# Where the tokens of a block are transposed, and a block more between a block and its experts, in the third layer of a graph network

## The chip, the cores and the metric

The program runs on one core of one Trainium2 chip. The metric is the device time of one execution in microseconds (us), the median over several. The core has five engines with queues of their own: TensorE (PE in the profile; PEld are its weight loads), VectorE (DVE), ScalarE (ACT), GpSimd (POOL) and SyncE (SP). They wait for one another by semaphores.

## The reference

6250 nodes with 256 features, 206250 edges sorted by target, 8 edge types. All is in fp32. The kernel computes

```
xn = layernorm(x)
h = xn
for l in 0, 1, 2:                      # graph network
    agg[r, n] = sum of h[src] over the edges of type r to node n
    h = einsum('rnd,rde->ne', agg, W[l]) + h @ root[l] + bias[l]
    h = relu(h) if l < 2 else sigmoid(h)
x = x + h + mixer(xn)                  # mixer: linear attention and an MLP
t = layernorm(x)
probs = softmax(t @ router.T); the two largest, scaled to sum 1, are combine
y = t + sum over 8 experts e of combine[e] * (gelu(t @ w1[e] + b1[e]) @ w2[e] + b2[e])
out = x + y
```

## The kernel before

**Tiles and stages.** The nodes are cut into 50 blocks (`window`) of 125. Before each layer a table of the nodes' features, already multiplied by the eight matrices of the edge types, lies in HBM; a layer is then a gather of rows and a sum by target. The first stage (phase 0) makes the table for layer 0; layers 0 and 1 make the next one, block by block. Layer 0 also does the mixer's projections, layer 1 its MLP, and layer 2, the third, the router and the experts.

**The gathers.** GpSimd issues one indirect DMA for each 128 edges (`nc.gpsimd.indirect_dma_start`, L517), 1612 a layer. Four of them are a chunk. Chunks go round in a ring of 8 slots in SBUF; before each chunk GpSimd waits on `slots_free`. SyncE turns landed halves of chunks into counts of `halves_ready`.

**A block's sum.** VectorE compares the edges' targets with the block's 125 nodes (`onehot`, L1022), and TensorE multiplies that with the gathered rows, four matrix products a chunk (`unit`, `add_tile` L1434). A block has seven units of fixed place, 0 to 6, and in a loop before the last one as many more as its edges need (`more_units`); the chunk of a block's last unit is also the first one of the next block. The first product of a unit frees the slot of the unit before it. When unit 6 is done VectorE adds what was computed beside it (`summing`, L1070).

**The third layer.** For the sum of block w: ScalarE takes the sigmoid as a tanh (`squash`, L795). VectorE adds the rest of the node, does the layer norm by Newton steps and gives the tokens `xhat` (`layer_out`, L1238 to L1251, semaphore `t_ready`). TensorE transposes them into `ps_tr` (`tokens_transposed`, which calls `transform`, L1377), ScalarE copies that to `hT` (L580). Then come the experts in six parts on TensorE (`experts(win, part)`): part 0 is the router's logits (L1689) and the up projections of experts 0 and 1 (L1699), parts 1 to 5 the other ups and the down projections (L1710), with the transposed combine weights (L1717) and the bias (L1722) among them. ScalarE does the router's exponential (L799), a Gelu for each half of an up projection (L810) and a table load at each change between Exp and Gelu; `warm` (L574) brings the Exp table early. VectorE finds the router's two largest (`largest_logit`, `router`, L1256 to L1279) and adds the experts into the block's output (`take`, L1289). ScalarE issues the store (L820).

**Order.** No scheduler is at work. Each engine runs its own queue in the order in which the code is written, so what stands behind a wait waits too. In block w of the third layer TensorE has unit 0, 1, 2, the transposes of block w-1, unit 3, part 0 of w-1, unit 4, parts 1 and 2, unit 5, parts 3 and 4, the extra units, unit 6, part 5. When the last block's units are done, `phase3_tail` does the last block's transposes and its six parts. ScalarE and VectorE have bodies of their own (`phase3`, `phase3_tail`), in which the work of block w-1 stands in the matching order.

Of the kernel before, what the change touches and what calls it, by code (L numbers as in the profile page):

```python
# [22 lines left out]
ACT = mybir.ActivationFunctionType  # L23
# [14 lines left out]
def gps_program(nc, t):  # L38
# [35 lines left out]
    with ExitStack() as ctx:  # L74
# [449 lines left out]
        def _(act):  # L524
# [252 lines left out]
            def phase3(cur, prev):  # L777
                w, parity, turn = cur
                load_base(2, w, parity)

                act.dma_start(xn_in[parity][:, :], rows(res_dram, w)).then_inc(xn_loaded[parity], 16)
                if w == 0 or w >= 2:
                    warm(ACT.Exp)
                if prev:
                    squash(prev)
                    copy_hT(3, prev)
                    logits_exp(prev)
                    gelus3(prev, range(E))
                    if w < NW - 1:
                        store_out(prev)  # L790

            def squash(win):

                act.wait_ge(summed, 2 * NW + win[0] + 1)
                nc.scalar.activation(h_sum[:, :], h_sum[:, :], ACT.Tanh, scale=0.5).then_inc(tanh_ready, 1)  # L795
# [25 lines left out]

            def experts(win):
                logits_exp(win)
                gelus3(win, range(E))
                store_out(win)

            def phase3_tail(win):
                warm(ACT.Exp)
                squash(win)
                copy_hT(3, win)  # L830
                logits_exp(win)
                store_out(window(win[0] - 1))
                gelus3(win, range(E))
                store_out(win)
# [6 lines left out]
        def _(dve):  # L841
# [388 lines left out]
            def layer_out(cur):  # L1230
# [4 lines left out]
                dve.wait_ge(tanh_ready, w + 1)  # L1235
                dve.wait_ge(xn_loaded[parity], turn * 16 + (16 + 2 * 16 * (NW // 2)))

                chain(nc.vector.scalar_tensor_tensor(out=fx[:, :], in0=h_sum[:, :], scalar=0.5,  # L1238
# [64 lines left out]
            def phase3(cur, prev, step):  # L1303
                step(3)
                if prev:
                    assert layer_out(prev) == P3_CHAIN
                step(4, 5)
                if prev:
                    largest_logit(prev)
                    router(prev)  # L1310
                    take(prev, range(0, 4))
                    take_b2(prev)
                step(6)
                if prev and cur[0] < NW - 1:
                    take(prev, range(4, E))

# [10 lines left out]
            def phase3_tail(win):  # L1327
                assert layer_out(win) == P3_CHAIN
                take(window(win[0] - 1), range(4, E))
                whole_block(win)  # L1330
# [4 lines left out]
        def _(pe):  # L1335
# [347 lines left out]
            def experts(win, part):  # L1683
# [9 lines left out]
                def up(e):  # L1693

                    if e >= 2:
                        pe.wait_ge(act_done, w * E + (e - 1))
# [55 lines left out]

            PARTS_BEHIND = {3: (0,), 4: (1, 2), 5: (3, 4), 6: (5,)}

            def phase3(cur, prev, unit):
                w = cur[0]
                for i in range(STATIC):
                    if i == STATIC - 1:
                        more_units(2, w)
                    unit(i)  # L1760
                    if prev and i == 2:
                        tokens_transposed(prev)
                    if prev:
                        for part in PARTS_BEHIND.get(i, ()):
                            experts(prev, part)

            def phase3_tail(win):
                tokens_transposed(win)
                for part in range(6):
                    experts(win, part)  # L1770
# [21 lines left out]
```

## Time and profile before

| | |
|---|---|
| three timed runs | 6509.38, 6512.33, 6513.76 us; median 6512.33 |
| profiled execution, first to last instruction | 8038.5 us |
| TensorE, products | 5658.1 us, 70% |
| GpSimd | 4625.1 us, 58% |
| VectorE | 2215.5 us, 28% |
| ScalarE | 1034.0 us, 13% |
| layer starts (first gather) | 386.8, 2853.1 and 5358.6 us |

The profiled execution has no other time than its span. It is 1526 us longer than the median, so it isn't a picture of the timed runs in every wait. Starts of TensorE's instructions are recorded, their ends are modelled. GpSimd's rows are the issues of gathers, not the transfers. A releaser called "remote" is one that the profile can't name, and "issue" is time in which it sees no wait at all.

### The profile page before, as it was taken

To read this page: it belongs to the slowest core of one execution; us is meant where nothing else is said; L and a number is where in the kernel's file an instruction comes from. 1 tells how busy PE (TensorE), PEld (TensorE's weight loads), DVE (VectorE), ACT (ScalarE), POOL (GpSimd) and SP (SyncE) were. 2 spreads that over 40 slices of the span, in tenths; PEclk is the share of its full clock that TensorE was granted. 3 is DMA by queue.
4 is the path that set the end of the run, shared out by engine and by line. 5 is a ranking of instruction groups with operands and counts; after the bars stand their busy time and mean duration, and the time that the engine had idled before them with its cause. 6 is when DMAs were issued, how large, how long until landed. Compare 5 with 4: busy or idle time off the path is not lost.

```text
span 8038.5 us, 86017 instructions
## 1 busy us (share of the span) xinstructions
PE 5658.1 (70%) x22890; PEld 4136.2 (51%) x22890; DVE 2215.5 (28%) x6194; ACT 1034.0 (13%) x2706; POOL 4625.1 (58%) x4920
## 2 busy tenths in 40 slices
PE   8946666666656677777777777766676666766667
PEld 3434444444444445555555555545565555555556
DVE  8711111111111122222222222213333333333333
ACT  2200000000001011111111111111111111111112
POOL 1166666666666656666666666655555555555554
PEclk9977887788778888888888888888888888888888
DMA  6633333333333344344444444443233333323332
GB/s 189 189 102 110 113 112 110 115 115 114 114 114 112 115 127 117 116 121 120 120 119 117 119 120 119 124 128 88 86 87 89 89 89 88 89 87 89 91 88 67
DMA packets 354391, 888.01 MB, mean 110 GB/s; under 512 B 86234, under 2 KB 179294, under 8 KB 335623
## 3 DMA queue, kind: packets, MB, share of 16 engines
q0 software_dynamic: 232080, 633.91, 26.9%
q10 hardware_dynamic: 114178, 243.16, 10.4%
q1 hardware_dynamic: 7740, 5.99, 0.2%
q8 instruction: 212, 3.47, 0.2%
q14 instruction: 181, 1.48, 0.1%
HBM read 697.11 MB, written 185.60 MB: 110 GB/s over the span
## 4 chain that ended last, share of the span: by engine, by line
PE 39%; another core or an unknown queue 32%; issue 15%; DVE 6%; ACT 4%; ACTq 2%; DVEq 1%; DMA 1%; POOL 0%; POOLq 0%; SPq 0%
PE ps_out L1434 16%; PE ps_y L1405 7%; PE ps_y L1699 4%; PE ps_b L1710 3%; PE ps_c L1710 2%; PE ps_tr L1614 2%; DVE r L1289 1%; DVE onehot L1022 1%; PE ps_b L1405 1%; PE ps_c L1405 1%; PE ps_c L1602 1%; ACT L810 1%; ACT L574 1%; PE ps_b L1602 1%
## 5 line engine op out<-in xcount | busy, mean ns | idle before, releaser
L517 POOL DMA_INDIRECT ring<-table,gather_idx x4836 | 4576.4, 946 | 3030.0 <-issue 1391.3
L1434 PE MATMUL ps_out<-ring,onehot 128*125 x8400 | 2148.6, 403 | 261.6 <-issue 221.5
L1434 PEld LDWEIGHTS ps_out<-ring,onehot 128*125 128x125 f32 x8400 | 1625.0, 200 | 653.8 <-issue 415.8
L1434 PE MATMUL ps_out<-ring,onehot_more 128*125 x2448 | 783.2, 476 | 832.0 <-DVE onehot_more L1022 596.0
L1405 PE MATMUL ps_y<-W,hT 128*125 128x512 f32 (+1 forms) x2400 | 1138.8, 615 | 170.9 <-issue 69.7
L1434 PEld LDWEIGHTS ps_out<-ring,onehot_more 128*125 128x125 f32 x2448 | 550.1, 236 | 1036.1 <-issue 937.8
L1405 PEld LDWEIGHTS ps_y<-W,hT 128*125 128x125 f32 x2400 | 496.2, 210 | 677.8 <-issue 552.1
L849 DVE COPY y_stage<-ps_y 125x512 f32<-125x512 f32 x150 | 103.6, 690 | 2174.5 <-remote 1231.6
L1022 DVE TENSOR_TENSOR onehot<-targets,ps_out 128x500 f32<-128x500 f32 x1050 | 647.2, 671 | 180.8 <-issue 138.8
L1022 DVE TENSOR_TENSOR onehot_more<-targets,ps_out 128x250 f32<-128x250 f32 x612 | 239.8, 414 | 1016.2 <-remote 416.7
L533 ACT COPY y_stage<-ps_y 125x512 f32<-125x512 f32 x350 | 201.1, 587 | 2455.3 <-PE ps_y L1405 1165.7
L1699 PE MATMUL ps_y<-hT,big 128*128 128x125 f32 x3200 | 472.3, 302 | 42.4 <-ACT gT L810 26.8
L1699 PEld LDWEIGHTS ps_y<-hT,big 128*128 128x128 f32 x3200 | 457.3, 217 | 76.9 <-issue 33.2
L1377 PE MATMUL ps_tr<-ident,xhat 125*128 125x125 f32 x100 | 32.7, 428 | 530.8 <-issue 436.9
L1710 PE MATMUL ps_b<-big,gT 128*125 128x256 f32 x800 | 243.2, 432 | 133.7 <-ACT gT L810 132.5
L810 ACT ACTIVATE gT<-ps_y,vectors 128x125 f32<-128x125 f32 x800 | 242.6, 363 | 600.3 <-PE ps_y L1699 401.5
L1377 PEld LDWEIGHTS ps_tr<-ident,xhat 125*128 125x128 f32 x100 | 14.1, 198 | 554.1 <-issue 453.9
L1289 DVE SCALAR_TENSOR_TENSOR r<-ps_c,combine,r 125x256 f32<-125x256 f32 x200 | 96.8, 484 | 564.7 <-remote 318.4
L1710 PEld LDWEIGHTS ps_b<-big,gT 128*125 128x125 f32 x800 | 157.7, 214 | 169.7 <-issue 142.4
L1289 DVE SCALAR_TENSOR_TENSOR r<-ps_b,combine,r 125x256 f32<-125x256 f32 x200 | 96.8, 484 | 536.3 <-PE ps_b L1710 149.7
L490 POOL TENSOR_TENSOR rstd<-mv,neg_half 125x1 f32<-125x1 f32 x50 | 33.4, 667 | 313.6 <-DVE mv L969 313.6
L1614 PE MATMUL ps_tr<-big,gT 128*125 128x256 f32 x800 | 187.4, 388 | 27.3 <-issue 27.1
(193 smaller groups left out, 3643.0 us busy)
## 6 DMA issues: line engine op xcount, KB each, us to landing
table<-y_stage ACTq DMA_DIRECT2D x147, 896.0 KB
ring<-table,gather_idx POOLq DMA_INDIRECT x4836
table<-y_stage ACTq DMA_DIRECT2D x147, 104.0 KB
xn_in<-xn_scratch ACTq DMA_DIRECT2D x100, 125.0 KB
base<-y_stage ACTq DMA_DIRECT2D x100, 125.0 KB
base_in<-base ACTq DMA_DIRECT2D x100, 125.0 KB
x_in<-in_x_dram ACTq DMA_DIRECT2D x75, 125.0 KB
xn_scratch<-xn_in ACTq DMA_DIRECT2D x50, 125.0 KB
```

What stands on the lines that cost most here:

```text
L517: nc.gpsimd.indirect_dma_start(ring[0:n, c * D:(c + 1) * D], None, table[l], bass.IndirectOffsetOnAxis(ap=gather_idx[0:n, tile:tile + 1].b ...
L533: nc.scalar.copy(y_stage[parity][:, b * 2 * D:(b + 1) * 2 * D], BANK[phase][b][0:WIN, 0:2 * D]).then_inc(y_evac_act, 1)
L810: last = nc.scalar.activation(gT[:, (e % GB) * K + f, :], ps_y[e % 2][:, f * WIN:(f + 1) * WIN], ACT.Gelu, bias=b1e[:, e, f:f + 1])
L849: nc.vector.tensor_copy(y_stage[parity][:, 2 * D:4 * D], BANK[phase][1][0:WIN, 0:2 * D]).then_inc(y_evac_dve, 1)
L1022: return nc.vector.tensor_tensor(out, targets[:, bass.ds(col, count)].unsqueeze(2).broadcast_to([128, count, n]), nodes.unsqueeze(1).broad ...
L1289: nc.vector.scalar_tensor_tensor(out=acc[parity][:, :], in0=(ps_b, ps_c)[e // 2 % 2][0:WIN, e % 2 * D:(e % 2 + 1) * D], scalar=combine[:, ...
L1405: last = nc.tensor.matmul(BANK[phase][b][0:WIN, 0:n], hT[parity][:, k, :], W[:, k, b * 2 * D:b * 2 * D + n], start=(k == 0), stop=(k == K ...
L1434: return nc.tensor.matmul(ps_out[w % 2][0:WIN, 0:D], lhsT, ring[:, bass.ds(slot + j * D, D)], start=first, stop=last)
L1602: last = nc.tensor.matmul(bank[:, (j % 4) * WIN:(j % 4 + 1) * WIN], W1[:, k, j * 128:(j + 1) * 128], xhatT[:, k, :], start=(k == 0), stop= ...
L1614: last = nc.tensor.matmul(ps_tr[0:WIN, D:2 * D], gT[:, j, :], W2[:, j, :], start=(j == 0), stop=(j == FJ - 1))
L1699: last = nc.tensor.matmul(ps_y[e % 2][:, f * WIN:(f + 1) * WIN], w1e[:, e, k, f * 128:(f + 1) * 128], hT[parity][:, k, :], start=(k == 0), ...
L1710: last = nc.tensor.matmul((ps_b, ps_c)[e // 2 % 2][0:WIN, e % 2 * D:(e % 2 + 1) * D], gT[:, (e % GB) * K + f, :], w2e[:, e, f, :], start=( ...
```

## The change

In the third layer a block now has two blocks in work beside its own sums: `win`, the block before, up to its transposed tokens, and `old`, the one before that, for its experts. On TensorE block w now has unit 0, part 0 of w-2, unit 1, part 1, unit 2, part 2, unit 3, part 3, the transposes of block w-1, unit 4, part 4, unit 5, part 5, the extra units, unit 6. On ScalarE `both_blocks` does the exponential and two experts' Gelus of the older block, the tanh of the newer, five experts, the copy of the transposed tokens, the last expert and the store. On VectorE it does the router of the older block, the layer norm of the newer, the takes. The layer norm waits for the transposes of the block before it, since `xhat` is one buffer. In the tail of each engine stand first both blocks, 48 and 49, and then the experts of block 49.

```
@@ scalar, phase3
-                if w == 0 or w >= 2:
+                old = window(w - 2) if w >= 2 else None
+                if w == 0:
                     warm(ACT.Exp)
                 if prev:
-                    squash(prev)
-                    copy_hT(3, prev)
-                    logits_exp(prev)
-                    gelus3(prev, range(E))
-                    if w < NW - 1:
-                        store_out(prev)
+                    both_blocks(old, prev)
+
+            def both_blocks(old, win):
+
+                if old:
+                    warm(ACT.Exp)
+                    logits_exp(old)
+                    gelus3(old, range(0, 2))
+                squash(win)
+                if old:
+                    gelus3(old, range(2, E - 1))
+                copy_hT(3, win)
+                if old:
+                    gelus3(old, range(E - 1, E))
+                    store_out(old)
...
             def phase3_tail(win):
-                warm(ACT.Exp)
-                squash(win)
-                copy_hT(3, win)
+                both_blocks(window(win[0] - 1), win)
                 logits_exp(win)
-                store_out(window(win[0] - 1))
                 gelus3(win, range(E))
                 store_out(win)
@@ vector, layer_out
                 dve.wait_ge(xn_loaded[parity], turn * 16 + (16 + 2 * 16 * (NW // 2)))
+                dve.wait_ge(tr_done, 2 * NW + w)
@@ vector, phase3
-                step(3)
-                if prev:
-                    assert layer_out(prev) == P3_CHAIN
-                step(4, 5)
-                if prev:
-                    largest_logit(prev)
-                    router(prev)
-                    take(prev, range(0, 4))
-                    take_b2(prev)
+                old = window(cur[0] - 2) if cur[0] >= 2 else None
+                step(3, 4, 5)
+                if prev:
+                    both_blocks(old, prev)
                 step(6)
-                if prev and cur[0] < NW - 1:
-                    take(prev, range(4, E))
+                if old:
+                    take(old, range(4, E))
+
+            def both_blocks(old, win):
+
+                if old:
+                    largest_logit(old)
+                    router(old)
+                assert layer_out(win) == P3_CHAIN
+                if old:
+                    take(old, range(0, 4))
+                    take_b2(old)
...
             def phase3_tail(win):
-                assert layer_out(win) == P3_CHAIN
-                take(window(win[0] - 1), range(4, E))
+                old = window(win[0] - 1)
+                both_blocks(old, win)
+                take(old, range(4, E))
                 whole_block(win)
@@ tensor, experts: up(e)
-                    if e >= 2:
+                    if w * E + e >= 2:
                         pe.wait_ge(act_done, w * E + (e - 1))
@@ tensor, phase3
-            PARTS_BEHIND = {3: (0,), 4: (1, 2), 5: (3, 4), 6: (5,)}
-
...
                     unit(i)
-                    if prev and i == 2:
-                        tokens_transposed(prev)
-                    if prev:
-                        for part in PARTS_BEHIND.get(i, ()):
-                            experts(prev, part)
+                    both_blocks(old, prev, i)
+
+            def both_blocks(old, win, i):
+
+                if old and i < 6:
+                    experts(old, i)
+                if win and i == 3:
+                    tokens_transposed(win)

             def phase3_tail(win):
-                tokens_transposed(win)
+                for i in range(6):
+                    both_blocks(window(win[0] - 1), win, i)
                 for part in range(6):
                     experts(win, part)
```

The first place is in the middle of the third layer on TensorE, around the transposes (`ps_tr`). Before, between two units (`ps_out`):

```order
L1434 MATMUL ps_out<-ring,onehot 125x256
L1377 MATMUL ps_tr<-ident,xhat 128x125 x2
L1451 ISA
L1434 ISA
L1434 MATMUL ps_out<-ring,onehot 125x256
```

Now, behind part 3 of the older block (ups `ps_y`, a down `ps_c`, the bias `ps_a`):

```order
L1708 MATMUL ps_y<-hT,big 128x125 x4
L1719 MATMUL ps_c<-big,gT 125x256 x2
L1731 MATMUL ps_a<-b2e,combT 125x256
L1708 MATMUL ps_y<-hT,big 128x125 x4
L1386 MATMUL ps_tr<-ident,xhat 128x125 x2
L1460 ISA
```

The transposes have moved from behind the third unit to behind the fourth and the older block's part 3.

The second place is the end of the program on TensorE, from the last unit's last product. Before:

```order
L1434 MATMUL ps_out<-ring,onehot 125x256
L1710 MATMUL ps_b<-big,gT 125x256 x2
L1710 MATMUL ps_c<-big,gT 125x256 x4
L1377 MATMUL ps_tr<-ident,xhat 128x125 x2
L1689 MATMUL ps_a<-vectors,hT 125x8 x2
L1699 MATMUL ps_y<-hT,big 128x125 x8
```

Now, from the same product; what is left out are parts 1 to 3 of block 48:

```order
L1443 MATMUL ps_out<-ring,onehot 125x256
L1698 MATMUL ps_a<-vectors,hT 125x8 x2
L1708 MATMUL ps_y<-hT,big 128x125 x8
L1719 MATMUL ps_b<-big,gT 125x256 x2
...
L1386 MATMUL ps_tr<-ident,xhat 128x125 x2
L1719 MATMUL ps_b<-big,gT 125x256 x2
L1708 MATMUL ps_y<-hT,big 128x125 x4
L1719 MATMUL ps_b<-big,gT 125x256 x2
L1719 MATMUL ps_c<-big,gT 125x256 x4
L1698 MATMUL ps_a<-vectors,hT 125x8 x2
L1708 MATMUL ps_y<-hT,big 128x125 x8
```

One block of experts stood behind the last unit but for three downs; now two whole ones stand there.

The third place is the end of the program on ScalarE. Before (`probs` is the router's exponential, `out_dram` the store):

```order
L574 ACT_TABLE_LOAD
L574 ACTIVATE act_warm<-zero_col 128x1
L795 ACTIVATE h_sum<-h_sum 125x256
L580 ACTIVATE hT<-ps_tr 128x2x125
L799 ACTIVATE probs,small<-ps_a,small 125x8
L820 DMA out_dram<-r_0 125x256
L810 ACT_TABLE_LOAD
```

Now, from block 48's first two experts on:

```order
L820 ACTIVATE gT<-ps_y,vectors 128x125 x4
L805 ACTIVATE h_sum<-h_sum 125x256
L820 ACTIVATE gT<-ps_y,vectors 128x125 x6
L825 COPY combT<-ps_a 8x125
L820 ACTIVATE gT<-ps_y,vectors 128x125 x4
L580 ACTIVATE hT<-ps_tr 128x2x125
L820 ACTIVATE gT<-ps_y,vectors 128x125 x2
L830 DMA out_dram<-r_0 125x256
L809 ACT_TABLE_LOAD
L809 ACTIVATE probs,small<-ps_a,small 125x8
L820 ACT_TABLE_LOAD
```

The tanh (`h_sum`) stands between Gelus and has no table load of its own; block 49's exponential has one, behind the store.

## Rows read from the trace of the kernel before

**Rows 1.** The page's section 1: busy time of each engine, share of the span, instructions
```profile
PE 5658.1 (70%) x22890; PEld 4136.2 (51%) x22890; DVE 2215.5 (28%) x6194; ACT 1034.0 (13%) x2706; POOL 4625.1 (58%) x4920
```

**Rows 2.** The page's section 5, GpSimd's gathers: count | busy, mean ns | idle before, releasers
```profile
L517 POOL DMA_INDIRECT ring<-table,gather_idx x4836 | 4576.4, 946 | 3030.0 <-issue 1391.3
```

**Rows 3.** Timeline, GpSimd, end of the third layer: start, length, what [idle before <-releaser]
```profile
7972.99 0.95 POOL L517 DMA_INDIRECT ring<-table,gather_idx  x1 [0.30 <-issue]
7977.26 0.94 POOL L517 DMA_INDIRECT ring<-table,gather_idx  x1 [3.32 <-remote]
```

**Rows 4.** Timeline, GpSimd, the first gather of each layer
```profile
386.76 1.22 POOL L517 DMA_INDIRECT ring<-table,gather_idx  x1 [11.29 <-issue]
...
2853.07 0.98 POOL L517 DMA_INDIRECT ring<-table,gather_idx  x1 [28.99 <-issue]
...
5358.59 0.97 POOL L517 DMA_INDIRECT ring<-table,gather_idx  x1 [30.83 <-issue]
```

**Rows 5.** Groups of instructions, GpSimd, 5358 to 7982, the third layer
```profile
L517 POOL DMA_INDIRECT ring<-table,gather_idx x1612 | 1525.2, 946 | 1128.9 <-issue 449.6 <-PE ps_out L1434 367.5 <-remote 311.8
```

**Rows 6.** Timeline, TensorE and VectorE, around one block's transposes
```profile
6602.84 1.89 PE L1710 MATMUL ps_c<-big,gT 128*125 128x256 f32 x8
...
6604.56 5.34 PE L1434 MATMUL ps_out<-ring,onehot 128*125 x24
...
6614.27 1.00 DVE L1289 SCALAR_TENSOR_TENSOR r<-ps_c,combine,r 125x256 f32<-125x256 f32 x2 [8.31 <-remote]
...
6622.03 0.68 PE L1377 MATMUL ps_tr<-ident,xhat 125*128 125x125 f32 x2 [12.12 <-issue]
```

**Rows 7.** Timeline, TensorE, one block at full clock
```profile
6684.65 2.04 PE L1710 MATMUL ps_b<-big,gT 128*125 128x256 f32 x4 [3.47 <-ACT gT L810]
...
6691.49 1.89 PE L1434 MATMUL ps_out<-ring,onehot 128*125 x8
...
6707.53 5.34 PE L1434 MATMUL ps_out<-ring,onehot 128*125 x24
```

**Rows 8.** Waits, 5800 to 7900: who <- for what: us in total, times, longest
```profile
PE ps_tr L1377 <- issue: 378.9, 32, 12.4
```

**Rows 9.** Timeline, all engines, the end of the program
```profile
8009.01 1.99 PE L1434 MATMUL ps_out<-ring,onehot 128*125 x8 [0.34 <-issue]
...
8015.71 0.44 PE L1377 MATMUL ps_tr<-ident,xhat 125*128 125x125 f32 x2 [2.12 <-DVE xhat L1245]
...
8016.71 0.57 PE L1689 MATMUL ps_a<-vectors,hT 128*125 128x8 f32 x4 [0.56 <-ACT hT L580]
...
8017.14 2.03 PE L1699 MATMUL ps_y<-hT,big 128*128 128x125 f32 x16
...
8018.23 0.17 DVE L1256 TENSOR_REDUCE small<-ps_a 125x1 f32<-125x8 f32 x1
8018.43 0.27 ACT L799 ACTIVATE probs<-ps_a,small 125x8 f32<-125x8 f32 x1 [1.86 <-DVE small L1256]
...
8018.80 1.28 ACT L810 ACT_TABLE_LOAD   x1
...
8020.10 1.13 ACT L810 ACTIVATE gT<-ps_y,vectors 128x125 f32<-128x125 f32 x4
...
8020.86 1.10 PE L1710 MATMUL ps_b<-big,gT 128*125 128x256 f32 x4 [1.70 <-ACT gT L810]
...
8032.40 1.89 PE L1710 MATMUL ps_c<-big,gT 128*125 128x256 f32 x8
...
8035.43 0.27 ACTq L820 DMA_DIRECT2D out_dram<-r  x1
```

**Rows 10.** Stretches: start:end, length, busy us (x) of PE, PEld, DVE, ACT, POOL, PEclk, DMA, GB/s
```profile
6614.00:6626.00 12.00, 3.97 (x11) 3.13 (x12) 7.33 (x22) 2.17 (x4) 8.47 (x9) 0.50 0.40 117
...
8011.00:8038.50 27.50, 18.91 (x117) 15.89 (x116) 12.58 (x42) 7.54 (x22) 0.00 (x0) 1.00 0.03 10
5700.00:7900.00 2200.00, 1533.89 (x7418) 1271.55 (x7417) 719.25 (x2101) 372.63 (x1002) 1279.05 (x1353) 0.83 0.31 89
```

More of the change, by code:

```diff
@@ L820, in store_out, with phase3_tail @@
                 act.dma_start(rows(t["out"], w), acc[parity][:, :]).then_inc(out_stored[parity], 16)
-            def experts(win):
+            def phase3_tail(win):
+                both_blocks(window(win[0] - 1), win)
                 logits_exp(win)
-                gelus3(win, range(E))
-                store_out(win)
-            def phase3_tail(win):
-                warm(ACT.Exp)
-                squash(win)
-                copy_hT(3, win)
-                logits_exp(win)
-                store_out(window(win[0] - 1))
                 gelus3(win, range(E))
@@ L1751, in experts @@
                         down(e)
-            PARTS_BEHIND = {3: (0,), 4: (1, 2), 5: (3, 4), 6: (5,)}
             def phase3(cur, prev, unit):
                 w = cur[0]
+                old = window(w - 2) if w >= 2 else None
                 for i in range(STATIC):
```

## The prediction

> **What bounds the kernel now.** I read the page first: TensorE is busy 5658.1 us of 8038.5, GpSimd 4625.1 [rows 1]. By that alone TensorE bounds the kernel. But the profiled span is 1526 us longer than the median of 6512.3 us, and no other time of that execution is given. So I first ask what in the trace is not in the timed runs.
>
> GpSimd issues all 4836 gathers, four to a chunk, and stands idle 3030.0 us between them [rows 2]. Its own timeline shows two kinds of gap: 0.30 us behind nearly every gather, so that one takes 0.95 + 0.30 = 1.25 us, and some longer ones, 3.32 us before the gather at 7977.26 [rows 3]. The long ones are waits for a free slot of the ring, which TensorE frees. The regular gaps are 4836 x 0.30 = 1451 us; the starts of the three layers are 11.3 + 29.0 + 30.8 = 71 us [rows 4]. What is left, 3030.0 - 1451 - 71 = 1508 us, are waits on TensorE. Take them out of the span: 8038.5 - 1508 = 6530 us, against 6512.3 measured. The timed runs are as long as the trace without a single one of these waits. From this I conclude that unprofiled the gathers' pace of 1.25 us bounds all three layers, and that TensorE's lateness belongs mostly to the profiled execution.
>
> The trace supports that where the wait of the third layer stands. TensorE's records end the last three experts' down projections at 6602.84 + 1.89 = 6604.7, and three units at 6604.56 + 5.34 = 6609.9; yet VectorE gets the last experts' result only at 6614.27, after 8.31 us of waiting for something unnamed, and the transposes begin at 6622.03, 12.1 us behind the units [rows 6]. Multiplications that the records price at 1.89 us have become about 9.5 us late. On its chain from there, VectorE and ScalarE need 6622.03 - 6614.27 = 7.8 us to make the tokens.
>
> The Trainium skill, "NOTIFIC — the notification-queue block", section 7.1, says that the block through which profiling records leave has a mode that stalls the engine producing them, "Stall the producer until software drains the ring", and that its inner pipeline always holds back rather than lose one. That would explain the lateness; by that rule it goes away unprofiled. No run here shows the mechanism.
>
> **TensorE against the gathers, third layer.** At full clock, from the first down projection of a block (6684.65) to the next block's first three units (6707.53) are 22.9 us, two extra units in it; those three units take 5.3 us [rows 7]. Transposes 0.44, the fourth unit 1.89, logits 0.57, two up projections 2.03 and the fifth unit 1.89 make 6.8 us [rows 7, 9]. Together 35.0 us. The chain of 7.8 us has 5.3 us of units beside it, so 2.4 us of real wait: 37.4 us a block. The gathers of a block take 1612 / 50 x 1.25 = 40.3 us. TensorE has 2.9 us a block to spare before the change, and eight chunks, 40 us of gathers, to even out its bursts.
>
> **The change part by part.**
> In blocks 2 to 49 of the third layer the transposes move from behind the third unit to behind the fourth and three quarters of the older block's experts. What waited 12 us there in the trace (378.9 us over the 32 waits of one kind that a stretch of 2200 us shows [rows 8]) now has about 15 us of other work in front. In the trace this is a large gain: the third layer's waits for slots are 1128.9 - 1612 x 0.30 - 30.8 = 614 us [rows 4, 5]. Unprofiled the 2.4 us a block go away behind a pace of 40.3 us that is not TensorE's: value 0. If the cover were gone (TensorE the bound), it would be worth 48 x 2.4 = 115 us; the bound from the other side is 0.
>
> VectorE builds two onehots before the router and no longer behind the tokens, and waits in addition for the previous transposes. Behind that new wait are the layer norm, the takes and the sixth onehot; the transposes that it waits for ended a whole block earlier: 0. ScalarE does two Gelu experts before the tanh; its table loads stay two a block, since the tanh stands behind Gelu without a load of its own: 0 in the loop. The bare move of the DMA store of an output block by one block is hidden by the alternating buffers: 0. GpSimd's and SyncE's queues have the same instructions in the same order.
>
> The end of the program has no gathers left to hide anything. Call U the end of the last unit, 8009.01 + 1.99 = 8011.0 in the trace; the span ends 27.5 us later, at 8038.5 [rows 9]. Before, three down projections stood there beside the last block's tanh and layer norm, and then one block of experts. Now TensorE has to do all of block 48's experts and then all of block 49's, and ScalarE and VectorE have both too:
> - U to block 48's first down projection. Logits 0.57 and two ups 2.03 are 2.6. The other way round, logits 0.57 and 0.3 to VectorE, then 8018.23 to 8020.86 (maximum, exponential, table load 1.28, Gelu) are 2.63 [rows 9]: 3.5 us. Block 49's layer norm runs under it.
> - From there to the last down projection's end, 8034.29 - 8020.86 = 13.4, and the transposes 0.44: 13.9 us.
> - Block 49's first down projection can't follow at once. ScalarE's queue has block 48's store in front of the exponential, and that waits for VectorE's last two takes: 8034.29 to 8035.70 are 1.4 us. A load of the Exp table follows, 1.28 us, which before was done early under TensorE's work. Then 8018.43 to 8020.86, 2.4 us. With the hand-over 5.2 us, under which TensorE's logits and first ups hide.
> - From there to the end of the span: 8038.5 - 8020.86 = 17.6 us.
> The sum is 3.5 + 13.9 + 5.2 + 17.6 = 40.2 us behind U, 27.5 before: +12.7 us.
>
> On that table load the Trainium skill, "ScalarE: Activation LUTs", section "What ACT_TABLE_LOAD costs", gives 1283 ns and a drain of about 1380 ns more for each switch. The trace has the 1.28 but lets the Gelu begin at 20.10, straight behind 18.80 + 1.28; the row decides. By the page the end would be an estimated 1.4 us longer.
>
> U itself. After the change TensorE has caught up before the last block ends: two extra units and the last one each wait for chunks 5 us apart and need 2.0. Where it waited long, the granted clock was 0.50 (1.2 GHz) between 6614 and 6626; over the last 27.5 us, with waits of about 2 us, it was 1.00 [rows 10]. At half clock the second half of the last unit and the first 2.6 us of experts would cost up to 3.5 us more; at full clock 0. Most of the last stretch is nearer to the second row; I take 1. Before the change TensorE is later in the last block by up to 2 us (five parts behind two units), so U may come that much earlier now: I take 0, keep -2. In all +13.7 us, between +10.7 and +16.2. On the profiled span alone the end would be 8052, but there the steady part falls; on the median it is 6512.3 + 13.7 = 6526.
>
> **Rivals.**
> A. The end is paid, but U comes 2 us earlier and the clock holds: +10.7 us, 6523, within 0.2%. For it: full clock through the end of the trace. Against it: TensorE's short work between chunks.
> B. Not slower: TensorE does bound part of the third layer. If a gather took 1.22 us unprofiled and not 1.25, the timed runs would hold 145 us of waits; by the trace's share of the third layer (614 of 1508) 59 us would lie there, and taking 2.4 us of each block's wait out of the way would return 60% of them, -35 + 13 = -22: 6490. It decides from TensorE's 37.4 us a block being above the gathers' time, which asks for a pace under 1.16, or for half clock in a fifth of the block. For it: the clock was 0.83 in the layer in the trace [rows 10]. Against it: the gaps of 0.30 never shrink, and the sum above closes within 18 us without any wait.
> C. The trace taken at its word, 379 us less for the third layer's wait: 6512 - 379 + 13 = 6146. Against it: 4836 x 1.25 = 6045 us of gathers, and 387 us before the first one [rows 4], are 6432 already. Impossible if the pace holds.
> D. The two blocks' experts at the end run at half clock throughout, or the moved order makes GpSimd wait: +13 for the order and +7 for a quarter of the engine's 27 us at half clock: 6532.
>
> **How the numbers follow.** Forecast 0.49, A 0.31, B 0.10, C 0.01, D 0.09. About 0.2%, 13 us, is what a measurement of this kernel can tell from no change. Slower by over 13.0 us (above 6525.4): most of the forecast's spread and D, less what of the forecast falls below, 0.52. Within: A and the rest, 0.38. Faster: B and C, 0.10. The range 6505 to 6537 takes in the bounds of the end and the weaker half of B; for the forecast alone it is 6522 to 6530.
>
> **What would show it.** In the profile of the changed kernel: the gathers' regular pace still 1.25; the wait before the transposes gone or under 2 us; the third layer's waits of GpSimd clearly under 614 us, and the profiled span so perhaps shorter by 100 us or more, while the median is longer; two runs of experts behind the last unit, 40 to 43 us from its end to the end of the span, an Exp load behind the store in ScalarE's queue between them. I am wrong if the median falls under 6500, since then TensorE was the bound unprofiled, or if the end is long and the median unchanged, since then there was a gain in the loop that I don't see.

## The result, and the profile after

| | us, median | lowest to highest | runs |
|---|---|---|---|
| before | 6512.25 | 6509.38 to 6515.15 | 12 |
| after | 6526.93 | 6523.42 to 6529.55 | 12 |

The ratio is 1.0023, with a 95% interval from 1.0015 to 1.0030: 14.7 us slower, where 6526 and +13.7 us were forecast. The profiled execution of after has a span of 6523.7 us, 3 us under its median, so here the profile is a picture of the timed runs. That of before was not, at 8038.5. Two groups of the page of after answer to [rows 1] and [rows 2]; the columns are the same.

```profile
PE 5464.6 (84%) x22890; PEld 3995.9 (61%) x22890; DVE 2201.3 (34%) x6194; ACT 1041.3 (16%) x2706; POOL 4631.4 (71%) x4920
```
```profile
L517 POOL DMA_INDIRECT ring<-table,gather_idx x4836 | 4582.9, 948 | 1520.8 <-issue 1466.0
```

A gather takes the same 0.95 us, but the idle time between gathers is 1520.8 us and not 3030.0. The difference is 1509 us; the prediction had counted 1508 us of waits for TensorE and taken them out of the sum. The page's chain of waits, which for before named TensorE with 39% of the span, now names the gathers (the row's end is left out):

```profile
POOL ring L517 54%; DMA ring<-table,gather_idx 9%; PE ps_out L1443 7%; PE ps_y L1414 3%; PE ps_y L1708 2%; DVE hT L980 1%; PE ps_b L1414 1%; PE ps_c L1414 1%; PE ps_b L1719 1%; PE ps_c L1719 1%; POOLq L510 0%; DMA table<-y_stage 0%; PE ps_t
```

The 1509 us must not be read as a gain of the change. The first experiment, a second profile of the kernel before, has none of them either.

**The end of the program.** This is the timeline of after on GpSimd, TensorE and ScalarE behind its last gather, and it answers to [rows 9]. Of two blocks' experts only the places that the prediction's sum uses are shown.

```profile
6477.31 0.90 POOL L517 DMA_INDIRECT ring<-table,gather_idx  x1 [0.30 <-issue]
...
6478.45 3.77 PE L1443 MATMUL ps_out<-ring,onehot 128*125 x8 [2.11 <-SPq L440]
6482.02 0.85 PE L1698 MATMUL ps_a<-vectors,hT 128*125 128x8 f32 x4
6482.72 2.87 PE L1708 MATMUL ps_y<-hT,big 128*128 128x125 f32 x16
6485.54 1.10 PE L1719 MATMUL ps_b<-big,gT 128*125 128x256 f32 x4
...
6494.46 0.38 PE L1386 MATMUL ps_tr<-ident,xhat 125*128 125x125 f32 x2
...
6497.29 1.89 PE L1719 MATMUL ps_c<-big,gT 128*125 128x256 f32 x8
6499.02 0.50 PE L1698 MATMUL ps_a<-vectors,hT 128*125 128x8 f32 x4
...
6504.36 1.45 PE L1719 MATMUL ps_b<-big,gT 128*125 128x256 f32 x4 [2.96 <-ACT gT L820]
6505.61 3.28 PE L1708 MATMUL ps_y<-hT,big 128*128 128x125 f32 x16
...
6517.54 1.89 PE L1719 MATMUL ps_c<-big,gT 128*125 128x256 f32 x8
```
```profile
6500.32 0.27 ACTq L830 DMA_DIRECT2D out_dram<-r  x1
6500.63 1.28 ACT L809 ACT_TABLE_LOAD   x1 [3.38 <-DVE r L1292]
6501.93 0.27 ACT L809 ACTIVATE probs<-ps_a,small 125x8 f32<-125x8 f32 x1
...
6502.30 1.28 ACT L820 ACT_TABLE_LOAD   x1
6503.60 1.13 ACT L820 ACTIVATE gT<-ps_y,vectors 128x125 f32<-128x125 f32 x4
```

The reader is to see two runs of experts behind the last unit, and between them the hole in TensorE's row: 2.96 us, in which it waits for ScalarE's first Gelu of block 49. In front of that Gelu ScalarE issues block 48's store, loads the Exp table, takes the exponential and loads the Gelu table, from 6500.32 on; the first part of this chain hides under TensorE's logits and ups. The products after the hole ran slowly, 3.28 us where [rows 9] has 2.03 for sixteen such instructions: the granted clock was 0.62 between 6504.3 and 6508.8, so partly at its lower level (1.2 GHz, called half clock below), and 1.00 from there to the last product.

### The profile page after: what moved, and what is told of

Same layout as the page of the kernel before. It is cut to its first block, busy times and chain, and to the rows that moved or that the text cites. A ratio compares the mean times of both kernels' runs of the same rounds, so it can differ in the third digit from the quotient of the medians.

```text
span 6523.7 us, 86066 instructions
## 1 busy us (share of the span) xinstructions
PE 5464.6 (84%) x22890; PEld 3995.9 (61%) x22890; DVE 2201.3 (34%) x6194; ACT 1041.3 (16%) x2706; POOL 4631.4 (71%) x4920
## 3 DMA queue, kind: packets, MB, share of 16 engines
q10 hardware_dynamic: 114178, 243.16, 12.6%
## 4 chain that ended last, share of the span: by engine, by line
POOL 54%; issue 18%; PE 15%; DMA 9%; DVE 2%; POOLq 1%; ACT 0%; DVEq 0%; ACTq 0%; SPq 0%
POOL ring L517 54%; DMA ring<-table,gather_idx 9%; PE ps_out L1443 7%; PE ps_y L1414 3%; PE ps_y L1708 2%; DVE hT L980 1%; PE ps_b L1414 1%; PE ps_c L1414 1%; PE ps_b L1719 1%; PE ps_c L1719 1%; POOLq L510 0%; DMA table<-y_stage 0%; PE ps_tr L1623 0%; PE ps_c L1611 0%; POOLq L315 0%
## 5 line engine op out<-in xcount | busy, mean ns | idle before, releaser
L517 POOL DMA_INDIRECT ring<-table,gather_idx x4836 | 4582.9, 948 | 1520.8 <-issue 1466.0
L1443 PE MATMUL ps_out<-ring,onehot 128*125 x8400 | 2324.0, 424 | 745.6 <-SPq L434 732.8
L1443 PEld LDWEIGHTS ps_out<-ring,onehot 128*125 128x125 f32 x8400 | 1669.3, 209 | 1250.5 <-issue 1004.1
L1414 PE MATMUL ps_y<-W,hT 128*125 128x512 f32 (+1 forms) x2400 | 1020.0, 565 | 24.5 <-DVE hT L980 12.1
L1443 PE MATMUL ps_out<-ring,onehot_more 128*125 x2448 | 702.6, 428 | 218.4 <-SPq L434 187.5
L1443 PEld LDWEIGHTS ps_out<-ring,onehot_more 128*125 128x125 f32 x2448 | 472.4, 206 | 418.3 <-issue 353.9
L1708 PE MATMUL ps_y<-hT,big 128*128 128x125 f32 x3200 | 416.6, 279 | 0.0
L1708 PEld LDWEIGHTS ps_y<-hT,big 128*128 128x128 f32 x3200 | 399.1, 193 | 27.7 <-issue 16.7
L580 ACT ACTIVATE hT<-ps_tr 128x250 f32<-128x250 f32 x150 | 57.2, 382 | 1000.8 <-PE ps_tr L1386 1000.8
L1719 PE MATMUL ps_c<-big,gT 128*125 128x256 f32 x800 | 197.4, 380 | 0.0
L980 DVE STREAM_TRANSPOSE hT<-xn_in 32x64 f32<-32x64 f32 x800 | 188.8, 236 | 15.0 <-PE ps_c L1414 3.0
```

Of the source, the lines that this page charges most:

```text
L517: nc.gpsimd.indirect_dma_start(ring[0:n, c * D:(c + 1) * D], None, table[l], bass.IndirectOffsetOnAxis(ap=gather_idx[0:n, tile:tile + 1].b ...
L980: last = nc.vector.transpose(hT_rows[parity][q * 32:(q + 1) * 32, :, n * 32:(n + 1) * 32], src[:, :, q * 32:(q + 1) * 32])
L1414: last = nc.tensor.matmul(BANK[phase][b][0:WIN, 0:n], hT[parity][:, k, :], W[:, k, b * 2 * D:b * 2 * D + n], start=(k == 0), stop=(k == K ...
L1443: return nc.tensor.matmul(ps_out[w % 2][0:WIN, 0:D], lhsT, ring[:, bass.ds(slot + j * D, D)], start=first, stop=last)
L1708: last = nc.tensor.matmul(ps_y[e % 2][:, f * WIN:(f + 1) * WIN], w1e[:, e, k, f * 128:(f + 1) * 128], hT[parity][:, k, :], start=(k == 0), ...
L1719: last = nc.tensor.matmul((ps_b, ps_c)[e // 2 % 2][0:WIN, e % 2 * D:(e % 2 + 1) * D], gT[:, (e % GB) * K + f, :], w2e[:, e, f, :], start=( ...
```

## The experiments

**1. The kernel before, profiled again.** No edit.

> The kernel before, unchanged, profiled once more. My theory: the waits of GpSimd for slots in the first profile belong to that profiled execution. If this one comes out without them, its span is near 6510 us, the gaps between gathers are 0.30 us in all three layers, the wait before the transposes is 0 to 2.4 us, and the span ends 31 to 34 us behind the last gather, against 46.4 in the changed kernel. Rival: the kernel before always has waits of about 600 us in its third layer when profiled and the change took them away; then the span is near 8040 again and the third layer has its 614 us.

One run of 6512.17 us, span 6510.0. From the page, its gathers; then the waits of TensorE between 4600 and 6400, where the third layer is steady (columns: who <- for what, us in total, times, longest), and the end of the program:

```profile
L517 POOL DMA_INDIRECT ring<-table,gather_idx x4836 | 4581.4, 947 | 1521.8 <-issue 1480.1
```
```profile
PE ps_out L1434 <- SPq L434: 205.3, 143, 4.4
PE ps_out L1434 <- DVE onehot L1022: 13.4, 37, 0.7
PE ps_tr L1377 <- DVE xhat L1245: 2.7, 1, 2.7
```
```profile
6477.81 0.90 POOL L517 DMA_INDIRECT ring<-table,gather_idx  x1 [0.30 <-issue]
...
6480.37 1.12 PE L1434 MATMUL ps_out<-ring,onehot 128*125 x4 [0.52 <-SPq L440]
...
6486.20 0.66 PE L1377 MATMUL ps_tr<-ident,xhat 125*128 125x125 f32 x2 [2.12 <-DVE xhat L1245]
...
6488.25 3.75 PE L1699 MATMUL ps_y<-hT,big 128*128 128x125 f32 x16
6491.80 1.67 PE L1710 MATMUL ps_b<-big,gT 128*125 128x256 f32 x4
...
6503.90 1.89 PE L1710 MATMUL ps_c<-big,gT 128*125 128x256 f32 x8
```

The idle time of the gathers, 1521.8 us, is that of after, 1520.8. The same stretch of after has the row below: TensorE waits for landed gathers (SPq L434 is the queue that announces them) as much as before, and at the transposes for nothing.

```profile
PE ps_out L1443 <- SPq L434: 218.7, 188, 3.9
```

So the wait of 12 us before the transposes [rows 6, 8], which the change was aimed at, is in one execution only. In the other it stands once in 45 blocks, with 2.7 us. The third layer's gathers run from 4461.36 to 6477.81 before, 2016.5 us, and from 4459.72 to 6477.31 after, 2017.6 us. In the unloaded variants below with either loop it is 2015.8 to 2019.0 us (experiments 2 to 5), so what the change moves in the loop is lost in that spread. From the last gather to the end of the span are 6510.0 - 6477.8 = 32.2 us before and 6523.7 - 6477.3 = 46.4 us after: 14.2 us, against 13.7 between the two spans and 14.7 between the medians.

One thing did change in the loop. For the same stretch, with the columns of [rows 10], before and after:

```profile
4600.00:6400.00 1800.00, 1567.44 (x7945) 1277.65 (x7945) 766.81 (x2240) 400.16 (x1077) 1361.66 (x1440) 0.94 0.40 115
```
```profile
4600.00:6400.00 1800.00, 1573.60 (x7912) 1288.62 (x7910) 751.79 (x2221) 391.97 (x1068) 1362.19 (x1438) 0.91 0.40 115
```

TensorE's granted clock fell from 0.94 to 0.91. It is so in all timed runs: 0.913 to 0.920 over the whole program after, 0.923 to 0.931 before. It cost nothing that the gathers' times show, and why it fell was not tried.

**2. The end alone.** The kernel before, in which only the last step is changed: block 48's experts stand behind the last unit, as after the change, and blocks 0 to 47 are left alone.

```
@@ scalar, phase3
-                    logits_exp(prev)
-                    gelus3(prev, range(E))
                     if w < NW - 1:
+                        logits_exp(prev)
+                        gelus3(prev, range(E))
                         store_out(prev)
...
@@ tensor, phase3
-                    if prev:
+                    if prev and w < NW - 1:
                         for part in PARTS_BEHIND.get(i, ()):
                             experts(prev, part)
@@ tensor, phase3_tail
-                tokens_transposed(win)
+                for part in range(6):
+                    experts(window(win[0] - 1), part)
+                    if part == 3:
+                        tokens_transposed(win)
                 for part in range(6):
                     experts(win, part)
```

What is left out moves ScalarE's and VectorE's work on block 48 in the same way.

> The kernel before with its old loop; only the experts of block 48 are taken out of the last block and done behind the last unit, in the order of the changed kernel's tail. Theory (the whole loss is the end of the program): +13 to +16 us against before, 6525 to 6528, as the changed kernel. Rival (part of the loss is in the loop, by the moved waits or the clock): less than +10 us, and the changed kernel stays slower than this one by the rest.

Measured: 6524.47 us (11 runs) against 6513.04 (21 runs), ratio 1.0019, interval 1.0010 to 1.0028, so +11.4 us (6.5 to 18). The end is 44.3 us long. Its timeline on TensorE:

```profile
6480.27 4.25 PE L1442 MATMUL ps_out<-ring,onehot 128*125 x8 [0.51 <-SPq L440]
...
6487.63 1.10 PE L1718 MATMUL ps_b<-big,gT 128*125 128x256 f32 x4 [0.79 <-ACT gT L810]
...
6506.44 1.10 PE L1718 MATMUL ps_b<-big,gT 128*125 128x256 f32 x4 [2.96 <-ACT gT L810]
6507.38 1.94 PE L1707 MATMUL ps_y<-hT,big 128*128 128x125 f32 x16
```

The hole is the same 2.96 us, but here the sixteen instructions behind it took 1.94 us and not 3.28, at full clock (1.00 granted between 6506.4 and 6509.2). The end alone makes most of the loss, and perhaps all: 11.4 and 14.7 lie in each other's intervals. The +11.4 us are 1.6 under the +13 to +16 that I expected, and above the 10 of the rival, part of the loss in the loop. In the profiles the two ends differ by 46.4 - 44.3 = 2.1 us, of which 1.3 are those sixteen instructions; the third layer's gathers take 2016.7 us here, 0.9 less than after. Whether the last 3 us between the medians are the clock or chance is open.

**3. Block 48 begun in the last block.** The kernel after, in which the first three of the six parts of block 48's experts stand in the last block ahead of its last unit.

```
     for i in range(STATIC):
         if i == STATIC - 1:
+            if w == NW - 1:
+                experts(prev, 0)
+                experts(prev, 1)
             more_units(2, w)
+            if w == NW - 1:
+                experts(prev, 2)
         unit(i)
...
```

ScalarE and VectorE have the matching order: behind block 47's store ScalarE does block 48's exponential and five of its experts.

> The changed kernel, its loop kept; in the last block parts 0, 1 and 2 of block 48's experts stand before the last unit, where TensorE waits for gathers (parts 0 and 1 behind block 47's last part, part 2 behind the extra units). Theory: 8 to 9 us of the 17.4 us of block 48's experts hide under the last gathers and the rest runs beside block 49's layer norm: +3 to +7 us against before, so 8 to 12 us less than the changed kernel. Rival (the end is bound by half clock or by the chain through ScalarE and VectorE and not by TensorE's queue): less than 4 us gained on the changed kernel.

Measured: 6523.99 us (11 runs), ratio 1.0018, interval 1.0009 to 1.0027: +11.0 us, and I had expected 3 to 7. TensorE's timeline, and ScalarE's of the same place:

```profile
6478.94 2.04 PE L1736 MATMUL ps_b<-big,gT 128*125 128x256 f32 x4 [3.05 <-ACT gT L824]
...
6483.24 1.89 PE L1460 MATMUL ps_out<-ring,onehot_more 128*125 x8
...
6489.84 1.89 PE L1460 MATMUL ps_out<-ring,onehot 128*125 x8
...
6505.19 1.16 PE L1736 MATMUL ps_b<-big,gT 128*125 128x256 f32 x4 [2.96 <-ACT gT L824]
```
```profile
6474.81 0.27 ACTq L834 DMA_DIRECT2D out_dram<-r  x1
6475.12 1.28 ACT L574 ACT_TABLE_LOAD   x1 [5.11 <-DVE r L1300]
...
6476.88 1.28 ACT L824 ACT_TABLE_LOAD   x1
6478.17 1.13 ACT L824 ACTIVATE gT<-ps_y,vectors 128x125 f32<-128x125 f32 x4
```

There are two holes now. The one before block 49's first down projection is still 2.96 us long, and a second one, 3.05 us, stands before block 48's, ahead of the last unit. That unit ends at 6491.7, 12.6 us behind the last gather (6479.16) and not 4.9. Behind it the end is 6524.5 - 6491.7 = 32.8 us and not 41.4: of 8.6 us won there 7.7 were lost ahead. This variant is 3 us under after (+11.0 and not +14.7 us against before), and the rival had said less than 4. I had taken the last block's slack for free. What stood in the way is what the rival named, the chain through ScalarE and VectorE: ScalarE's queue waits 5.11 us for VectorE's last takes of block 47, to store it, before it can begin block 48. So the last block's slack on TensorE went into waiting for that queue.

**4. The table load ahead of the store.** The kernel after, at the end of the program only.

```
                     gelus3(old, range(E - 1, E))
+                    if win[0] == NW - 1 and last:
+                        warm(ACT.Exp)
                     store_out(old)
...
             def phase3_tail(win):
-                both_blocks(window(win[0] - 1), win)
+                both_blocks(window(win[0] - 1), win, True)
```

> The changed kernel; at the end ScalarE loads the Exp table ahead of block 48's store and not behind it. Theory: the load hides under the wait for VectorE's takes; from the store's issue to block 49's exponential 0.1 to 0.4 us are left of 1.61, and from the last gather to the end of the span 1.3 us less than the changed kernel's 46.4. Rival (the exponential waits for the logits anyway): no change. One time can't tell 1.3 us; the rows do.

One run, 6521.5 us, span 6519.3; the end is 43.7 us long, with the last gather at 6475.58.

```profile
6501.66 1.10 PE L1721 MATMUL ps_b<-big,gT 128*125 128x256 f32 x4 [1.68 <-ACT gT L822]
6502.60 1.95 PE L1710 MATMUL ps_y<-hT,big 128*128 128x125 f32 x16
```

The hole is 1.68 us, 1.28 less than 2.96: exactly the load. That is the term that the prediction had put into its 5.2 us. The end is 2.7 us shorter than after's and not the 1.3 that I expected, since behind this hole the products ran at full clock: from the first down projection to the end of the span are 6519.3 - 6501.66 = 17.6 us, as in [rows 9], and 19.3 in after.

**5. TensorE kept busy in the hole.** The edit of experiment 4, and six products without use in what is left of the hole (experts of block 49, behind part 0).

```
+                    if part == 0:
+                        for _ in range(6):
+                            nc.tensor.matmul(ps_tr[0:WIN, D:2 * D], Wx[:, 0, 0:WIN], Wo[:, 0, :],
+                                             start=True, stop=True)
```

> The kernel after the change with two edits at the end of the program: the Exp table is loaded ahead of block 48's store (as in the kernel with that edit alone, whose end was 43.7 us long in one profile), and six products without use stand in TensorE's wait before block 49's first down projection, so that it doesn't idle there. My theory (the end adds up from the chain, and the clock gives back at most 1.5 us): end 42.5 to 43.7 us behind the last gather, about 6522 to 6524, 3 us under after (6527) and 10 above before. Rival (the end's cost is TensorE's clock and the table load): it comes back to within 5 us of before, 6517 or less.

Measured: 6526.20 us (11 runs) against 6511.64 (15 runs), ratio 1.0022, interval 1.0013 to 1.0031, nearly after's own. Its end is 43.9 us long.

```profile
6502.54 2.75 PE L1788 MATMUL ps_tr<-Wo,Wx 128*125 128x256 f32 x12
...
6505.14 1.03 PE L1722 MATMUL ps_b<-big,gT 128*125 128x256 f32 x4
```

Six products are twelve instructions and 2.75 us, not the 1.6 us that I had counted, so they filled the hole and held the first down projection up: it begins 1.5 us behind the first Gelu (6503.62), in experiment 4 0.8 us behind it (6500.90). The end is 2.5 us shorter than after's in the profile, but the median is only 0.7 lower, within its spread; I had expected 6522 to 6524. So a shorter end in one profile is not shown to be a shorter timed run, at this size. The rival, that table load and clock make the loss, expected 6517 or less and is excluded: 14.6 us are still there.

**6 and 7. TensorE as the bound.** Both kernels with 36 products without use in each of the third layer's blocks 2 to 49.

```
 before:                                          after:
         for part in PARTS_BEHIND.get(i, ()):             both_blocks(old, prev, i)
             experts(prev, part)                 +        if w >= 2 and i == 2:
+        if w >= 2 and i == 4:                   +            for _ in range(36):
+            for _ in range(36):                 +                nc.tensor.matmul(... as above)
+                nc.tensor.matmul(... as above)
```

> The kernel before, with 36 products of 256 columns a block added on TensorE behind the fifth unit in the third layer's blocks 2 to 49; their results go to an unused half of a PSUM bank. They only take TensorE's time, about 36 x 0.26 = 9.3 us a block at full clock, to make TensorE the bound of that layer. My theory (the order is worth 2.4 us a block where TensorE bounds and nothing where the gathers do): TensorE needs 35.0 + 9.3 + 2.4 = 46.7 us a block against the gathers' 40.3, so 48 x 6.4 = 307 us, less 40 us that the ring of eight chunks evens out: about +265 us, 6780 (6740 to 6820). The wait before the transposes, seen once in 45 blocks without the load, stands in nearly every block. Rival (nothing waits there even where TensorE bounds): 46.7 - 2.4, so about 6665 and no wait.

> The kernel after the change with the same 36 products a block on TensorE, behind the third unit in the third layer's blocks 2 to 49. My theory: the wait before the transposes is hidden, so TensorE needs 44.3 us a block: 48 x 4.0 = 192, less 40, plus 14 for the end: about 6512 + 166 = 6680, and so some 100 us (80 to 120) under the loaded kernel before. Rival: if the move is worth nothing in the loop even with TensorE as the bound, it stays 14 us above the loaded kernel before.

Measured: 7054.46 us (7048.55 to 7055.96, 4 runs) and 6950.06 us (6948.37 to 6952.81, 4 runs), beside 6511.64 for the kernel before. Both levels are far above the 6780 and 6680 that I expected, since a product costs 0.44 us and not 0.26. But the difference is 104.4 us, and 80 to 120 were expected. The loaded kernel before, TensorE's group for the load, its waits between 4900 and 6700, and one block's transposes:

```profile
L1769 PE MATMUL ps_tr<-Wo,Wx 128*125 128x256 f32 x2500 | 545.3, 379 | 0.0
```
```profile
PE ps_tr L1378 <- DVE xhat L1246: 93.5, 35, 2.7
...
PE ps_out L1435 <- SPq L435: 0.2, 1, 0.2
```
```profile
5500.70 15.71 PE L1769 MATMUL ps_tr<-Wo,Wx 128*125 128x256 f32 x72
...
5540.28 0.43 PE L1378 MATMUL ps_tr<-ident,xhat 125*128 125x125 f32 x2 [2.65 <-DVE xhat L1246]
```

And the loaded kernel after, the waits of the same stretch:

```profile
PE ps_b L1720 <- ACT gT L821: 38.3, 35, 1.4
PE ps_out L1444 <- DVE onehot L1025: 10.9, 30, 0.7
...
PE ps_out L1444 <- SPq L435: 0.3, 1, 0.3
```

TensorE no longer waits for gathers (SPq: 0.2 us in 1800), so it is the bound. Now the wait before the transposes is there in each of the 35 blocks, 93.5 / 35 = 2.67 us, and the change takes all of it away. It puts a smaller one in its place: the first down projection of the older block waits 38.3 / 35 = 1.09 us for its Gelu. By these two waits that is 1.58 us a block; by the medians it is 104.4 / 48 = 2.18. In the traces the time from one block's transposes to the next block's is 51.62 us in the loaded kernel before and 49.28 in the loaded kernel after, as the mean over blocks 4 to 47: 2.34 us a block. Of these, TensorE's idle time gives 1.70 (3.28 and 1.58) and the products themselves 0.63 (48.33 and 47.70 us busy). The granted clock of the two stretches is 0.99 and 1.00; that this is the reason is likely and not shown. 48 x 2.34 = 112 us is more than 104, since the end costs the change time here too: 64.8 us behind the last gather before, 74.8 after.

**8. A small load.** The loaded kernel before with 6 products instead of 36.

> The kernel before with only 6 of the added products a block on TensorE, behind the fifth unit in the third layer's blocks 2 to 49: by the loaded kernels' profiles (0.44 us a product at full clock) 2.6 us a block, about as long as the wait that the change hides. My theory (TensorE has more than that to spare in a block, the gathers set the pace): within 3 us of before, 6509 to 6516, though 48 x 2.6 = 126 us of work are added; the idle time of TensorE before its units falls by about as much as the products take. Rival (TensorE bounds the third layer already, so taking or adding 2.6 us a block moves the time): 6570 to 6640.

Measured: 6529.52 us (11 runs) against 6524.45 for the kernel before in the same rounds (15 runs), ratio 1.0007, interval 0.9998 to 1.0016: +5 us, between -1 and +10. The kernel before itself took 12 us more in these rounds than in the others, so only the ratio is used. 126 us of added work cost that little. In the profile the third layer's gathers take 2023.0 us, 6.5 more than in the kernel before; 4.5 and 4.3 us more stand in the first two layers as well, where nothing was changed, so some 2 us are left for the load. The waits, in the stretch of the first experiment:

```profile
PE ps_out L1435 <- SPq L435: 112.9, 58, 4.1
PE ps_tr L1378 <- DVE xhat L1246: 41.7, 17, 2.9
```

TensorE's wait for gathers fell from 205.3 to 112.9 us. The wait for the tokens showed itself in 17 of 45 blocks, 41.7 us where there were 2.7, and that too is hidden behind the gathers' pace. I had expected the idle time to fall by what the products take. The two waits together fell by 53 us only, though the products' own row in that stretch has 121 us: TensorE's busy time rose from 1567 to 1620 us, at a granted clock of 0.97 where it had been 0.94. With more to do the engine got more of its full clock, and the rest of its work took less time: the products of the sums were busy 823 us in that stretch, and 885 in the kernel before. Five us above before is a little more than the 3 that I had allowed, and I can't tell it from none. The rival, TensorE as the bound already, expected 58 us or more and is excluded.

## Why the prediction was right

- **The profile of before was not what is timed.** Right. The prediction took 1508 us out of the span; the second profile of the same kernel has 1508 us less idle time at the gathers (3030.0 - 1521.8). The experiments show that the lateness isn't in the timed runs; what makes it was not tried.
- **The gathers' pace bounds the loop, so the hidden wait is worth 0.** Right, and shown from both sides: the third layer's gathers took 2016.5 us before and 2017.6 after, 126 us of added work moved the time by 5, and with TensorE as the bound the move gave 2.34 us a block, 112 in 48 blocks, near the 48 x 2.4 = 115 us named as the other bound. The wait itself was sized right, 2.4 us and 2.67 measured.
- **TensorE's spare time.** Mis-sized. The prediction summed 35.0 us a block "at full clock" and found 2.9 us to spare. In the loaded kernel before, where the clock is full (0.99), a block took 1800 / 35 = 51.4 us; less the load of 15.7 and the wait of 2.7 leaves 33.0. So 40.3 - 33.0 - 2.7 = 4.6 us were to spare. [Rows 7] isn't at full clock at its start: a granted 0.65 from 6684.6 to 6688.8, where the first four and the next sixteen products took 2.04 and 2.44 us, and the loaded kernel has 1.03 and 1.95 for them. The remaining 0.6 come from adding lengths that overlap the next start (6.8 us, where the loaded kernel has 6.2). In the kernel as it is timed the clock in the loop is 0.94, a block's busy time 35.1 us and its idle time 5.2, so the 35.0 is near what happens, but by luck. Of the forecast only rival B's condition hung on it.
- **The end behind the last unit.** The terms were 3.5, 13.9, 5.2 and 17.6. The trace of after has 6485.54 - 6482.22 = 3.3 (the last unit ends at 6478.45 + 3.77), 6499.18 - 6485.54 = 13.6, 6504.36 - 6499.18 = 5.2, and 6523.66 - 6504.36 = 19.3: 41.4 us, forecast 40.2. In the second profile of before the same stretch is 6510.0 - 6481.49 = 28.5, so the difference is 12.9 us, forecast 12.7. That this is so close is partly luck: both ends are about 1 us longer than the forecast had them, and for the same reason. After, the last term was 1.7 too small, by products behind the hole at half clock; in experiments 2 and 4, where that place had full clock, it measures 17.7 and 17.6. Before, block 49's logits and first ups ran at half clock (3.75 us for sixteen instructions, 0.53 granted between 6486.2 and 6493.4), where [rows 10] had 1.00 throughout.
- **The end of the last unit itself.** Forecast +1, at most +3.5. It lies 4.9 us behind the last gather after and 3.7 us before: +1.2. After, its eight instructions took 3.77 us, the half clock that the prediction feared (0.57 granted between 6478.4 and 6485.5); before, they came in two halves of 1.12 us, at a granted 1.00.
- **The rivals.** B (a gain in the loop) is excluded by the time of the third layer's gathers and by the small load. C (the trace at its word) is far off. A and the forecast differ by 3 us, less than a measurement tells; the last unit at half clock speaks for the forecast. D saw half clock rightly, but counted it for after alone. The mean granted clock from the last unit on is 0.88 after (6478 to 6523) and 0.88 before (6481.5 to 6510), so it is a small part of the difference.

## What to carry to other kernels

A wait that the profile shows on an engine is worth its length only where that engine sets the pace. Compare the profiled span with the timed median first; where they differ, profile once more before a wait is believed. A step that moves work one block later leaves the loop as long as it was, but puts a block's work behind the end, where nothing hides it. Here that cost 11 to 15 us and gained nothing; with the engine made the bound, the same step gave 104 us, the cost of the end taken off.

## What the runs showed of the hardware

- Two profiled executions of one kernel can differ by 1528 us in span (8038.5 and 6510.0), while all its timed runs on record lie between 6507.8 and 6529.1 us.
- The same hole of 2.96 us in TensorE's work was followed by half clock in two kernels (3.28 us for sixteen instructions after, 3.56 in experiment 3) and by full clock in another (1.94 us in experiment 2). I did not find what tells them apart.
- TensorE's granted clock rose with its work: 0.94 in the third layer of the kernel before, 0.97 with 6 products more a block and 0.99 with 36. So 121 us of added products made it only 52 us busier.
- A gather of 128 rows holds GpSimd for 0.95 us, and 0.30 us pass to the next one: 1612 of them take 2016.5 us, 1.25 each, in the kernel before and after alike.
- A load of ScalarE's table takes 1.28 us, and the Gelu begins 0.02 us behind it (6502.30 + 1.28, 6503.60). Moved out of the way, it shortened TensorE's wait by 1.28 us.
- An fp32 product of 256 columns by 128 rows is two instructions in the trace, and 0.44 us at full clock (15.71 us for 36). My first price of 0.26 us was that of one of the two (1.03 us for four in a row).
